# Mixture of experts after a state-space block: routed tiles gathered by a slot table and added onto the shared rows by accumulating DMAs

## The reference

```
scores = softmax(xf @ gate_w.T)                    # 8 experts
topk_w, topk_idx = top_k(scores, 2); topk_w /= sum(topk_w)
h1 = einsum('th,ehi->tei', xf, w1); h3 = einsum('th,ehi->tei', xf, w3)
y = einsum('tei,te,eih->th', silu(h1) * h3, combine, w2)
shared = (silu(xf @ sw1) * (xf @ sw3)) @ sw2
return y + shared                                  # added to the image
```

## Time and profile before

| | |
|---|---|
| time, median of 3 runs | 2801.65 us (2800.4 to 2802.36) |
| the profiled execution | 2802.32 us, span 2800.7 us |
| PE busy | 2437.4 us (87%) |
| DVE busy | 1409.5 us (50%) |
| POOL busy | 1127.7 us (40%) |
| ACT busy | 1012.9 us (36%) |
| DMA queues | q1 (SP) 138.79 MB, q0 (POOL) 80.23 MB |

### The profile page before, as it was taken

One profiled execution on the slowest core, in us unless ns is written; L12 is line 12 of the kernel. 1 busy time (PEld: TensorE's weight loads), 2 busy tenths in 40 slices (PEclk: granted clock), 3 DMA queues, 4 the chain that ended last, 5 costly groups with the idle time before them and its releaser, 6 DMA issues.

```text
span 2800.7 us, 28349 instructions
## 1 busy us (share of the span) xinstructions
PE 2437.4 (87%) x7648; PEld 1257.2 (45%) x7649; DVE 1409.5 (50%) x1767; ACT 1012.9 (36%) x1971; POOL 1127.7 (40%) x959
## 2 busy tenths in 40 slices
PE   5788888878888888877999999999999999999962
PEld 3345445444444444444444444444444444444431
DVE  1899999998999999996321111111111111111125
ACT  3776766776667767762100100010011001100000
POOL 2788787787787887874003400000000000000015
PEclk7999999999999999999999999999999999999985
DMA  9212112212122222222024311230202202030026
GB/s 297 71 66 68 64 62 68 66 66 70 60 66 69 66 63 71 66 68 72 28 103 131 117 34 39 97 112 22 112 22 112 112 23 112 26 116 23 22 71 211
DMA packets 92975, 220.27 MB, mean 79 GB/s; under 512 B 11217, under 2 KB 34361, under 8 KB 89537
## 3 DMA queue, kind: packets, MB, share of 16 engines
q1 hardware_dynamic: 77840, 138.79, 15.2%
q0 software_dynamic: 15024, 80.23, 8.1%
HBM read 172.25 MB, written 46.73 MB: 78 GB/s over the span
## 4 chain that ended last, share of the span: by engine, by line
PE 56%; DVE 25%; issue 10%; ACT 5%; POOL 2%; DVEq 1%; DMA 0%; ACTq 0%; SPq 0%; POOLq 0%
PE pair L1442 31%; DVE WALL L1005 15%; PE single L1454 15%; DVE pair L988 8%; PE pair L1323 4%; PE single L1229 2%; PE pair L1224 2%; ACT z L818 1%; POOL WALL L614 1%; PE pair L1424 1%; ACT WALL L770 1%; DVEq L270 1%; PE single L1291 1%; PE pair L1316 0%; DVE X L948 0%
## 5 line engine op out<-in xcount | busy, mean ns | idle before, releaser
L1442 PE MATMUL pair<-WALL,z 128*128 (+1 forms) x1952 | 855.0, 596 | 31.0 <-ACT z L818 29.6
L527 POOL TENSOR_TENSOR WALL<-WALL 128x768 f32<-128x768 f32 x384 | 696.5, 1816 | 243.5 <-DVE WALL L1005 229.2
L1005 DVE TENSOR_TENSOR_SCAN WALL<-WALL,carry,pair 128x384 f32<-128x384 f32 x640 | 613.4, 1000 | 20.5 <-ACT WALL L770 4.2
L1323 PE MATMUL pair<-WALL,ident 128*128 128x384 f32 x1536 | 581.1, 504 | 3.1 <-DVE pair L988 3.1
L1442 PEld LDWEIGHTS pair<-WALL,z 128*128 128x128 f32 x1952 | 366.4, 190 | 483.4 <-issue 480.1
L1127 DVE TENSOR_TENSOR dtu<-dt,pair 128x512 f32<-128x512 f32 x122 | 83.9, 688 | 803.2 <-ACT dt L824 797.1
L770 ACT ACTIVATE WALL<-dt,An 128x384 f32<-128x384 f32 x768 | 424.1, 605 | 75.0 <-DVE WALL L1005 56.5
L988 DVE TENSOR_TENSOR pair<-dtu,pair 128x768 f32<-128x768 f32 x384 | 368.8, 960 | 51.8 <-POOL dtu L456 15.8
L824 ACT ACTIVATE dt<-pair 128x512 f32<-128x512 f32 x122 | 72.8, 597 | 828.4 <-PE pair L1442 828.4
L1323 PEld LDWEIGHTS pair<-WALL,ident 128*128 128x128 f32 x1536 | 293.9, 198 | 138.2 <-issue 22.1
L594 POOL DMA_DIRECT2D WALL<-in_L_ffn_w_dram x21 | 13.9, 666 | 826.3 <-PE single L1454 824.7
(11 more groups left out here) (213 smaller groups left out, 2037.9 us busy)
## 6 DMA issues: line engine op xcount, KB each, us to landing
WALL<-crows SPq DMA_DIRECT2D x192, 384.0 KB, 3.4
WALL<-in_L_ffn_w_dram POOLq DMA_DIRECT2D x24, 2048.0 KB, 13.5
u<-xrows SPq DMA_DIRECT2D x61, 256.0 KB
xrows<-zrow SPq DMA_DIRECT2D x43, 256.0 KB, 2.7
yrows<-expx SPq DMA_DIRECT2D x31, 256.0 KB
yrows<-onex SPq DMA_DIRECT2D x30, 256.0 KB
WALL<-in_L_ffn_sw_dram POOLq DMA_DIRECT2D x3, 2048.0 KB, 13.0
X<-in_x_dram SPq DMA_DIRECT2D x4, 1152.0 KB, 7.8
```

What stands on the lines that cost most here:

```text
L527: pool.tensor_tensor(hC[m], hs[:, (NS * j + n) % HRING, :, :], Cs[G % 3][:, n % CG, :].unsqueeze(1).to_broadcast([P, HALF, T]), ALU.mult). ...
L1005: scan = nv.tensor_tensor_scan(hs[:, m, h, :], dA[(NS * j + n) % AHEAD][:, h, :], Dt[:, h, 0:T], init, ALU.mult, ALU.add)
L1323: last = mm(Yt[:, h, 0:T], ident[:, :], hC[n % RING][:, h, :], start=(n == 0), stop=(n == NS - 1))
L1442: last = mm(bank[2 * w + q][:, :], xT[k][:, r, :], WALL[:, ds(off + (w * RR * I + r * I + q * 512), 512)], start=(r == 0), stop=(r == RR - 1))
```

## The change

- `xrows` and `yrows` have 2304 + 128 spare rows and no routed part. The zero stores go; one store of a zeroed `yd` to the spare rows of each comes.
- A table `slots` in DRAM has for each of the 43 x 128 routed places a token and a weight. It is preset with spare tokens and weight 0. After `places`, POOL scatters (token, weight) pairs to it, 8 bytes a row, 48 indirect DMAs of 96 rows, loads it back as `tab` (128 x 43 x 2) and casts the tokens to `tabi`.
- A routed tile's x is gathered by POOL from `xrows` by the tile's column of `tabi` (`gather`), in place of SP's load. Its y is added by POOL to `yrows` at the same tokens, by an indirect DMA with an add (`add_rows`), in place of SP's store; each add waits until the one before has landed. The order on POOL is gather(t+2), add(t), gather(t+3), add(t+1).
- DVE's `gate` multiplies in a routed tile by the slot's weight too, so that y needs none later.
- ACT makes `xT_copy(t+1)` ahead of `y_copy(t-1)` in every tile from tile 2 on.
- The weight loads move from POOL to SP: the first two of the shared ones behind x at the start, expert 1's behind `store_tile(7)`, the others behind the last shared store, with the waits that POOL had.
- The last stage: SP loads 4 images of rows from `yrows` (`ysum`), PE transposes 24 chunks through 8 banks, DVE adds them, SP stores half images. No gathers, no weighting.

The core of the diff:

```diff
 # SP
+            for dst, src in weights_of(0, WS0)[0:2]:
+                sp.dma_start(dst, src).then_inc(s_w, 16)
...
-            with sp.Fori(SHT, NT) as t:
-                sp.dma_start(xrows[ds(t * P, P), :].rearrange("p (r c) -> p r c", r=RR),
-                             zrow[:, :].unsqueeze(1).to_broadcast([P, RR, P])).then_inc(s_zero, 16)
...
-            with sp.Fori(0, SHT // 2 - 1) as t2:
+            with sp.Fori(0, SHT // 4) as t2:
                 two_tiles(t2)
...
+            sp.wait_ge(r_done, 1)
+            for dst, src in weights_of(1, WS1):
+                sp.dma_start(dst, src).then_inc(s_w, 16)
+            with sp.Fori(SHT // 4, SHT // 2 - 1) as t2:
+                two_tiles(t2)
+            for t in range(SHT - 2, SHT):
                 store_tile(t, t % 2)
...
+            sp.wait_ge(t_add[0], 16 * ((RTT + 1) // 2))
+            sp.wait_ge(t_add[1], 16 * (RTT // 2))
...
+            for b in range(B):
+                sp.dma_start(ysum[b], yrows[b * PIX:(b + 1) * PIX, :].rearrange("(j q) c -> q j c", j=JC)).then_inc(c_ld[b], 16)
+            for b in range(B):
+                for half in range(2):
+                    sp.wait_ge(c_x, b * JC + (half + 1) * (JC // 2))
+                    lo, hi = half * (H // 2), (half + 1) * (H // 2)
+                    sp.dma_start(out[b:b + 1, :, lo:hi, :].rearrange("a (c r) h w -> c (a r) (h w)", r=RR),
+                                 X[:, b * RR:(b + 1) * RR, lo * W:hi * W]).then_inc(c_out, 16)
 # POOL
+            for g in range(NCH):
+                for s in range(2):
+                    pool.indirect_dma_start(
+                        out=slots, out_offset=bass.IndirectOffsetOnAxis(ap=dsti[:, s, g:g + 1], axis=0),
+                        in_=pk[:, s, g, :], in_offset=None).then_inc(r_sc, 16)
...
+            def gather(t, k):
+                pool.wait_ge(t_xps, t - 1)
+                on_a_count()
+                pool.tensor_copy(gix[:, k:k + 1], tabi[:, ds(t - SHT, 1)]).then_inc(r_gix, 1)
+                pool.wait_ge(r_gix, t - SHT + 1)
+                on_a_count()
+                pool.indirect_dma_start(out=xin[k], out_offset=None, in_=xrows,
+                                        in_offset=bass.IndirectOffsetOnAxis(ap=gix[:, k:k + 1], axis=0)).then_inc(t_g[k], 16)
+            def add_rows(t, k):
+                after(pool, t_add[1 - k], (t - SHT + k) * 8)
+                on_a_count()
+                pool.tensor_copy(aix[:, k:k + 1], tabi[:, ds(t - SHT, 1)]).then_inc(r_aix, 1)
+                pool.wait_ge(t_y, t + 1)
+                pool.wait_ge(r_aix, t - SHT + 1)
+                on_a_count()
+                pool.indirect_dma_start(out=yrows, out_offset=bass.IndirectOffsetOnAxis(ap=aix[:, k:k + 1], axis=0),
+                                        in_=yout[k], in_offset=None, compute_op=ALU.add).then_inc(t_add[k], 16)
 # ACT, tile()
                 silu(t, 0)
                 silu(t, 1)
-                if behind:
-                    y_copy(t - 1, 1 - k)
                 if ahead:
                     xT_copy(t + 1, 1 - k)
+                if behind:
+                    y_copy(t - 1, 1 - k, routed)
 # DVE, gate() and places()
+                    nv.scalar_tensor_tensor(out=act[q], in0=sil[q], scalar=tab[:, ds(t - SHT, 1), 1], in1=bank[2 + q][:, :],
+                                            op0=ALU.mult, op1=ALU.mult).then_inc(t_act, 1)
+                    link(nv.tensor_scalar(q4i, dsti[:, s, :], P.bit_length() - 1, None, ALU.logical_shift_right))
+                    link(nv.tensor_scalar(mx, mx, float(RTT), None, ALU.mult))
+                    link(nv.scalar_tensor_tensor(out=dsti[:, s, :], in0=q4i, scalar=-float(P * RTT - 1), in1=mx,
+                                                 op0=ALU.mult, op1=ALU.add))
 # PE, last stage
+                for r in range(RR):
+                    last = te.transpose(bank[g % 8][:, r * CP:(r + 1) * CP], ysum[b][:, j, r::RR], ident[0:CP, 0:CP])
```

More of the change, by code:

```diff
@@ L400, in store_image @@
[L400 to L406, removed]
+            for q in range(2, E + 1):
+                if q == 2:
+                    sp.wait_ge(t_yps, SHT)
+                else:
+                    sp.wait_ge(t_yps, sp.value_load(endt[0:1, q - 3:q - 2], min_val=SHT, max_val=NT))
+                sp.wait_ge(s_w, 32 + 48 * (q - 1))
+                sp.sem_inc(s_sp_passed, 1)
+                for dst, src in weights_of(q, (WS0, WS1)[q % 2]):
+                    sp.dma_start(dst, src).then_inc(s_w, 16)
@@ L409, in _ @@
+            sp.wait_ge(c_out, 32 * B)
         @block.gpsimd
@@ new lines, in _ @@
+            for t in range(SHT, SHT + 2):
+                gather(t, t % 2)
+            gather(SHT + 2, 0)
+            for k in range(2):
+                pool.wait_ge(t_out[k], 16 * (SHT // 2))
+            add_rows(SHT, 0)
+            gather(SHT + 3, 1)
+            add_rows(SHT + 1, 1)
+            with pool.Fori(SHT // 2 + 1, (NT - 3) // 2) as t2:
+                for k in range(2):
+                    gather(2 * t2 + k + 2, k)
+                    add_rows(2 * t2 + k, k)
+            gather(NT - 1, 0)
@@ L620, in _ @@
+            for t in range(NT - 3, NT):
+                add_rows(t, t % 2)
         @block.scalar
@@ L857, in _ @@
             tile(2, 0, True, True)
-            with sc.Fori(1, (NT - 3) // 2) as t2:
+            with sc.Fori(1, SHT // 2 - 1) as t2:
                 tile(2 * t2 + 1, 1, True, True)
                 tile(2 * t2 + 2, 0, True, True)
-            tile(NT - 2, 1, True, True)
-            tile(NT - 1, 0, True, False)
-            y_copy(NT - 1, 0)
+            for t in range(SHT - 1, SHT + 3):
+                tile(t, t % 2, True, True)
+            with sc.Fori(SHT // 2 + 1, (NT - 3) // 2) as t2:
+                tile(2 * t2 + 1, 1, True, True, True)
+                tile(2 * t2 + 2, 0, True, True, True)
+            tile(NT - 2, 1, True, True, True)
+            tile(NT - 1, 0, True, False, True)
+            y_copy(NT - 1, 0, True)
         @block.vector
@@ L1133, in actT_copy, with tile @@
                 nv.tensor_copy(actT[q].rearrange("p k t -> p (k t)"), bank[5 + q][:, :]).then_inc(t_aT, 1)
-            def tile(t, between=None):
-                gate(t, 0)
-                gate(t, 1)
+            def tile(t, between=None, routed=False):
+                gate(t, 0, routed)
+                gate(t, 1, routed)
                 if between:
@@ L1467, in act_transpose, with tile @@
                     last.then_inc(t_aps, 1)
-            def tile(t, k, routed, behind=True, ahead=True, after_routed=None, with_counts=False):
+            def tile(t, k, routed, behind=True, ahead=True, after_routed=None, with_counts=False, next_routed=None):
                 up(t, k, routed)
                 if ahead:
-                    x_transpose(t + 1, 1 - k)
+                    x_transpose(t + 1, 1 - k, routed if next_routed is None else next_routed)
                 if behind:
```

216 lines of the change are left out of this document (79 added, 137 removed).

## The result

The kernel after took 2762.9 us, median of 4 runs (2761.42 to 2764.9); the kernel before, in the runs beside it, 2801.34 us (2800.4 to 2802.36). The ratio is 0.9863, 95% interval 0.9846 to 0.988: faster by 38.4 us. Forecast were 82 us. The sign was right and the time lies in the range, but less than half of the gain came, so one of the terms was badly wrong.

A forecast was written before the change was run, and what follows sets the result against it. The prediction took VectorE to bound the scan, PE the tiles (with a hole from ScalarE's order), and GpSimd's gathers the last stage. 0.3 - 38 + 10 + 0 - 54 = -82 us, from 2802.3 to 2720; range 2702 to 2765.

The forecast's parts named there:

- Start: Start and scan stage: GpSimd's extra work before the semaphore leaves 0 to 0.3 us on the path, +0.3 us.
- ScalarE's order: Tile stage: xT_copy ahead of y_copy closes PE's hole, 22.02 us a tile instead of 22.70; gain 38 us, bounds 20 and 39.
- the hole doesn't close: Rival, tile stage: register loads and waits before the up product hold PE, half of 38 us stays, 2739 us; chance 0.12.
- Routing: Routing beside the tiles: 48 slot scatters take GpSimd 60 us from 1436 on and stay hidden, cost 0.
- Expert 1's weights: Tile 9: the load of tile 10 queues behind the weights, PE stalls 8.7 us once; +10 us, bounds 5 and 13.
- Gathers and adds: Routed tiles: gathers land in time behind adds of 3 us, also beside weights; 0 us, bounds 0 and 21.
- weights delay the gathers: Rival, routed tiles: one row in each packet gives 18 turns, gathers 2.1 us late 7 times, 2735 us; chance 0.14.
- The add holds the software queue: Rival, tiles from 21 on: 40 gathers stand behind slow adds, each 7.7 us late, 3028 us; chance 0.08.
- Last stage: After the last down product: add, image loads and stores end at D+39.5 instead of D+93.8; -54 us, bounds -62 and -44.

The follow-up runs named there:

- e1_order: The kernel before with only ScalarE's order changed, the copy of xT ahead of the copy of y in every tile: 2763.8 us against 2802.4, ratio 0.986.
- e4_load_ahead: The kernel after with SyncE's load of tile 10 issued ahead of expert 1's weights, tile 8's store behind them: 2752.33 us, ratio 0.9824.
- e7_wide: The kernel after with waits after each pair of slot scatters, plus 48 unbroken scatters of 64-byte rows behind the table: 2761.73 us, ratio 0.9862.
- e8_mended: The kernel after with waits after each pair of slot scatters, tile 10's load ahead of expert 1's weights, gathers one tile earlier: 2708.56 us, ratio 0.9665.

## Why the prediction was wrong, point by point

- **Start, +0.3.** Up(2) began 2.3 us later in after, but e1_order, whose start is that of before, has +2.3 too, and e4_load_ahead and e7_wide begin tile 0 at 1315.55 and 1315.72. It is scatter between executions, mostly of how long PE keeps the lower clock in tile 0 (granted clock from 1320 to 1325 us: 1.00 in before, 0.65 in after). Nothing was added that can be told from it.
- **ScalarE's order, -38.** Right. The period was forecast at 22.02 and is 21.92, because the up product's 13.83 in the earlier trace rows still had PE's start after the hole in it; without a hole it is 13.74. That is 58 x 0.105 = 6.1 us more; the tile with the counts takes 1.7 us more than its neighbours instead of 1.3, which leaves 5.7. Most of it (4.8 us) is lost again in five tiles that 0.8 us less of period makes late. Alone it measured -38.6, and -44.8 with the late loads mended. The rival that the hole doesn't close, by register loads and waits, is out.
- **Routing, 0. This is the step that failed.** It priced the 48 slot scatters correctly (0.92 us and 0.30 of gap, 58.5 us in all, hidden with 200 us to spare) and took it that work hidden on GpSimd costs the others nothing. It measured +37.4 us in tile 6 and 38.6 in the time when the stream was broken up. The rows to doubt it with stood in the earlier trace rows: before issued its scatters in twos with waits between them (13.4 us once, 70.2 us in all for landings), and the change takes those waits away. The prediction used these rows as a price for one scatter and not for the rate at which scatters may follow each other. In the scatter loop of before that was one every 3.2 us, and the fastest long row of indirect DMAs in the trace was the last stage's, one every 1.64 us; the new one, 1.22 us, is faster than both, so the trace of before doesn't cover it, and a bound from above was due there as it was for the add. What the stream loads is not known; that it holds the other engines is.
- **Expert 1's weights, +10.** Right in mechanism and nearly in size: 8.3 us, of which the wait past the wanted time is 5.9 (forecast 8.7) and the lower clock the rest (2.3; forecast 1.3). The load landed at +19.7 after the up product's start instead of +22.5.
- **Gathers and adds, 0 (bounds 0 to 21).** Six tiles late by 6.6 us. 4.8 of them belong to the shorter period, as e1_order shows with loads of rows; the change adds 1.7. With the gathers issued a tile earlier 7.4 us came back (2724.3 - 8.3 - 2708.6). The landing beside weights was forecast at +11.5 and the wish at +13.9; measured +14.2 in tile 24 (up at 1892.22, x transposes at 1906.39) against +13.7. The gather was issued at +3.6, no later than forecast (+4), though the add's issue takes 1.58 us and not 1.24; the time went in the queue. The prediction counted 10 turns for add and gather, with two rows in each packet of both. That holds for the gather; the add's 128 rows are 128 packets (the lines of e8_mended's section), so there are 9 + 5 = 14 turns. By the prediction's own 0.69 us a turn that is an estimate of 2.5 + 9.7 + 2 = +14.2, which is what was measured. The rival by which weights delay the gathers, with one row in each packet, was right for the add and so half right in mechanism: 6 times, 1.1 us each instead of 2.1.
- **The add holds the software queue (rival, 3028 us).** Out: 4.9 us for an add, 3.6 for the gather behind it, and a plain store in its place changes nothing in the runs' times. The Trainium skill's rule cited in the prediction (*Collectives: The Full Stack*, "The bandwidth ceiling: the fold count and why AG ≠ RS ≠ AR": on a ring of three or more ranks the reducing collective gets half the copying one's rate, because the add reads two sources) is about collectives. Here the direction is the same, 4.9 us to landing against 2.7, but the add also has 144 packets against 80, and no run tells the two apart.
- **Last stage, -54.** -50.7; the end came at D+43.1 and not at D+39.5. The add was down at D+6.3 (forecast 5.5), the four image loads at D+26.0 (forecast 22). The moved bytes from 2716 to 2761 in slices of 1.1 us show why:

```profile
GB/s 0 0 0 0 29 89 115 13 140 291 279 209 248 218 220 233 233 233 231 235 211 253 244 209 233 237 340 376 372 373 370 373 371 372 371 374 364 160 19 0
```

  Loads, alone and beside the first stores, run at 209 to 291 GB/s, stores alone at 340 to 376. So loads were over-rated (305 was taken) and stores under-rated (295), and together they came 3.6 us later.

The sum by the runs' spans: -37.2 (e1_order's span against before's, its start and its five late tiles in it) + 37.4 + 8.3 + 1.7 - 50.3 (up(60) to the end against e1_order's) = -40.1, and the two spans differ by 40.05.

## What to carry to other kernels

An engine that is off the critical path can still stop the others by how it issues. When a change takes the waits out of a loop of indirect DMAs, its rate of issue is a new quantity: look for the highest rate that the trace has shown, and where the new one is above it, put a pause of a microsecond after every two or keep the wait. And when the profile of a change disappoints while each engine is as busy as forecast, list one repeated event and take differences: a single long period among sixty shows what no share of busy time does.

## What the runs showed of the hardware that was not expected

- 48 indirect DMAs issued by GpSimd at one every 1.17 to 1.23 us slowed PE to one matmul every 2.80 us mostly, 24 to 38 us after the stream's start, and held ScalarE for up to 49.6 us; 27 to 41 us were lost each time (scatter and gather, 8 and 64 bytes, 32 and 96 rows). At one every 1.41 us 1.5 us were lost, at one every 1.6 us nothing. 48 plain DMAs at one every 0.50 us did no harm.
- A pause of 3.1 us in the stream gave PE back for about 10 us only.
- An indirect DMA with an add took GpSimd 1.58 us to issue for 128 rows of 2 KB against 1.01 without, and landed 4.9 us after issue against 2.7. It moved as 144 packets against 80: one row in a packet instead of two.
- Issue hardly depends on the number of rows: 0.87 us for 32 rows of 8 bytes, 0.92 for 96.
